# Values of the second attention for seven batches projected beside the first layer's routing, with the expert weights in other buffers and GpSimd splitting the context

## What is computed

```python
x = x + L0_attention(layernorm(x), ctx)            # 16 heads of 16
x = x + L0_experts(layernorm(x))                   # top 1 of 8 experts, 256 -> 1024 -> 256
x = x + L1_attention(layernorm(x), ctx, mask)      # 8 heads of 64, a null key and value
x = x + L1_experts(layernorm(x))                   # top 8 of 64 experts and a shared one
# inside L1_attention:
k, v = split(ctx @ Wkv, 2)                         # 361 x 512 each, per batch
q = l2norm(stable_layernorm(x) @ Wq) * q_scale
k = l2norm(k) * k_scale                            # per head; v is used as it is
```

## Time and profile before

| | |
|---|---|
| time, median of 3 runs | 731.22 us (730.6 to 733.69) |
| time of the profiled execution | 732.75 us |
| span of the profiled execution | 731.0 us |
| PE busy | 638.7 us (87%) |
| DVE busy | 391.9 us (54%) |
| ACT busy | 400.2 us (55%) |
| POOL busy | 242.0 us (33%) |
| moved by DMA | 65.11 MB, mean 89 GB/s |

### The profile page before, as it was taken

The page is one execution under the profiler, slowest core; times in us unless marked ns, Lnnn a source line. Parts: engine busy times, 40 slices in busy tenths (PEclk is TensorE's granted clock), DMA queues, the critical chain, the costliest instruction groups (busy, mean ns, idle before and its releaser), DMA issues.

```text
span 731.0 us, 15087 instructions
## 1 busy us (share of the span) xinstructions
PE 638.7 (87%) x4762; PEld 512.4 (70%) x4763; DVE 391.9 (54%) x1171; ACT 400.2 (55%) x952; POOL 242.0 (33%) x307
## 2 busy tenths in 40 slices
PE   3999889999751989998999999998696999999995
PEld 2877566666450888976878666665464999999995
DVE  5222467777643111118898745555774665566662
ACT  1454689989641333245667788686331555545442
POOL 5011455555218000001110000000044787787771
PEclk9999599999955999999999999999599999999999
DMA  6118000000086388403120010000106645555552
GB/s 146 46 31 270 7 2 2 2 2 2 1 263 214 121 282 264 149 32 85 32 53 1 8 42 1 1 2 1 32 14 170 180 141 159 155 144 148 144 143 67
DMA packets 66838, 65.11 MB, mean 89 GB/s; under 512 B 10424, under 2 KB 60373, under 8 KB 66662
## 3 DMA queue, kind: packets, MB, share of 16 engines
q1 hardware_dynamic: 62204, 58.06, 26.5%
q0 software_dynamic: 1824, 4.32, 2.3%
q10 hardware_dynamic: 2762, 2.11, 1.0%
HBM read 56.17 MB, written 8.29 MB: 88 GB/s over the span
## 4 chain that ended last, share of the span: by engine, by line
PE 69%; ACT 10%; DVE 7%; issue 5%; DMA 3%; POOL 3%; SPq 2%; DVEq 1%; POOLq 0%; ACTq 0%
ACT probs L767 4%; PE psum L1119 4%; PE psum L1106 4%; PE psum L2218 3%; PE psum L2166 3%; PE psum L2168 3%; PE psum L2167 3%; PE psum L615 3%; PE psum L629 3%; PE psum L1593 3%; PE psum L706 3%; PE psum L1615 3%; PE psum L1602 3%; DMA v_all<-in_L_ffn_W_dram 3%; PE psum L696 2%
## 5 line engine op out<-in xcount | busy, mean ns | idle before, releaser
L767 ACT ACTIVATE probs<-probs,negmax 100x361 f32<-100x361 f32 x128 | 68.9, 587 | 10.7 <-POOL probs L812 10.6
L820 DVE TENSOR_SCALAR_CACHE_REDUCE probs<-psum 100x361 f32<-100x361 f32 x128 | 60.7, 531 | 19.4 <-PE psum L696 19.4
L706 PEld LDWEIGHTS psum<-ident,probs 100*128 100x128 f32 (+1 forms) x384 | 40.4, 159 | 27.6 <-issue 20.4
L706 PE MATMUL psum<-ident,probs 100*128 100x100 f32 (+1 forms) x384 | 48.9, 266 | 11.2 <-ACT probsT L775 4.8
L1147 ACT ACTIVATE kT_all<-psum,kT_all 128x128 f32<-128x128 f32 x88 | 25.2, 369 | 51.6 <-PE psum L1106 51.6
L812 POOL TENSOR_SCALAR probs<-probs 100x722 f32<-100x722 f32 x64 | 50.5, 789 | 5.1
L2347 POOL TENSOR_TENSOR we_low<-v_all,we_high 128x512 fp32r<-128x512 f32 (+1 forms) x34 | 46.0, 1373 | 17.1 <-ACT we_high L2271 12.7
L1106 PE MATMUL psum<-kT_all,v_all 128*128 128x128 f32 x352 | 43.3, 283 | 8.5 <-DMA v_all<-in_L_ffn_W_dram 3.4
L2166 PE MATMUL psum<-xT_high,we_high 128*128 128x400 f32 x128 | 45.2, 353 | 5.5 <-DVE v_all L2411 4.1
L1106 PEld LDWEIGHTS psum<-kT_all,v_all 128*128 128x128 f32 x352 | 42.1, 198 | 11.2 <-issue 7.0
L2057 POOL TENSOR_TENSOR xT_low<-kT_all,xT_high 128x1600 fp32r<-128x1600 f32 x1 | 3.6, 3567 | 131.1 <-ACT xT_high L2034 131.1
(11 more groups left out here) (420 smaller groups left out, 1691.5 us busy)
## 6 DMA issues: line engine op xcount, KB each, us to landing
v_all<-in_L_ffn_W_dram SPq DMA_DIRECT2D x16, 1024.0 KB, 7.8
kT_all<-coefT_dram SPq DMA_DIRECT2D x18, 400.0 KB, 3.7
v_all<-in_L_ffn_Wg_dram SPq DMA_DIRECT2D x34, 128.0 KB, 2.2
v_all<-in_L_ffn_Wu_dram SPq DMA_DIRECT2D x34, 128.0 KB, 2.3
v_all<-in_L_ffn_Wd_dram SPq DMA_DIRECT2D x34, 128.0 KB, 2.3
ctx_nat<-in_ctx_dram SPq DMA_DIRECT2D x16, 192.0 KB, 2.5
xs_dram<-zeros SPq DMA_DIRECT2D x1, 2048.0 KB, 7.7
rank_rows<-rank_dram SPq DMA_DIRECT2D x18, 100.0 KB, 3.0
```

Of the source, the lines that this page charges most:

```text
L706: last = nc.tensor.transpose(pT_ps[0:rows[t], t, hh * NQ:(hh + 1) * NQ], probs[:, n % NPB, hh, t * P:t * P + rows[t]], ident[0:NQ, 0:NQ])
L767: last = nc.scalar.activation(row, row, ACT.Exp, bias=negmax[:, n % NPB, hh:hh + 1])
L820: last = nc.vector.tensor_scalar(probs[:, n % NPB, hh, 0:NKV], psum[0:NQ, n % 2 * 2 + hh, 0:NKV], -CLAMP, None, ALU.max, ALU.max, accum_ou ...
```

## The change

The value products of batches 0 to 6 move from the projections into the end of attention 0 and into the gate (`early_values`); batch 7 stays (`last_values`). They write straight to their final place in `v_all`, so the expert weights, which stood there, move to the key and query buffers (W2 in two halves). The context transposes now number sixteen instead of eight: 0 to 7 and one more before the experts (contexts 0 to 6 for values, then context 0 again for keys, then context 7 for values), and seven in the projections (contexts 1 to 7 for keys). The list `CTX1` holds this order.

Wkv is loaded at the very start and split by POOL during the first stages. In the gate POOL splits contexts 1, 2 and 3 of the list and Wq, ahead of the scatter; DVE splits 0 and 4 to 8. In the projections POOL splits all, from a full copy that ACT makes as well (`ctxT_full`), and DVE none. SP issues the biases and the weights of two experts first, then context 4, eight small transfers of the null value, and contexts 5 to 10. ACT loads the first rows (`act_first_rows`) after five batches' values and seven contexts.

```diff
 
     xnT1_ps = psum[:, 7, 0:2 * NQ].rearrange("p (c n) -> p c n", c=2)
     k1_ps = psum[:, 2:5, :]
-    v1_ps = [psum[:, k, :] for k in (6, 5, 6)]
+    CTX1 = list(range(B - 1)) + [0, B - 1] + list(range(1, B))
+    CTX_V, CTX_K = [*range(B - 1), B], [B - 1, *range(B + 1, 2 * B)]
+
+    def v1_ps(b, t):
+
+        return psum[:, t + 2 if b < B - 1 else (6, 5, 6)[t], :]
 
     def kT1_ps(b, t):
 
-        return psum[:, t % 2 + 5 if 3 * b + t < 3 * B - 4 else (3 * b + t) % 2, :]
+        return psum[:, (3 * b + t) % 2 + 5, :]
     q1_ps = psum[:, 7, :]
 
...
 
-    def sp_ctx1(sp, b, p):
-
+    def sp_ctx1(sp, n):
+
+        b, p = CTX1[n], n % 2
+        sp.wait_ge(ctxT_in_psum, CTX0 + max(n - 1, 0))
         sp_ctx(sp, b, p)
...
@@ -755,9 +770,37 @@
             b, s = m // QUADS0, m % QUADS0
             if b > 0 and s in finish:
                 finish[s](b - 1)
+            if m == M0 - 2:
+                pe.wait_ge(A0.clipped, 2 * M0)
+                transpose_ctx1(pe, 0)
         weighted(M0 - 1)
-        for s in range(3):
-            finish[s](B - 1)
+        transpose_ctx1(pe, 1)
+        finish_transpose(B - 1)
+        early_values(pe, 0, 0, 0, 3)
+        finish_transpose_back(B - 1)
+        early_values(pe, 0, 0, 3, 5)
+        early_values(pe, 0, 1, 0, 1)
...
+
+        p, cols = n % 2, slice(t * P, t * P + rows[t])
+        products = ((ctxT_high, high, 0), (ctxT_high, low, 0), (ctxT_low, high, 0), (ctxT_high, low, 1), (ctxT_low, high, 1))
+        for k in range(first, end):
+            part, w, c = products[k]
+            last = nc.tensor.matmul(ps, part[p][:, c, cols], w[:, c, :], start=(k == 0), stop=(k == 4))
+        return last
+
+    def early_values(pe, b, t, first=0, end=5):
+
+        if first == 0:
+            pe.wait_ge(ctxT_split, CTX_V[b] + 1)
+            pe.wait_ge(w1x_split, 2)
+            if b > 0:
+                pe.wait_ge(v1_stored, 3 * (b - 1) + t + 1)
+        last = times(v1_ps(b, t)[0:rows[t], :], CTX_V[b], t, wv1_high, wv1_low, first, end)
+        if end == 5:
+            last.then_inc(v1_in_psum, 1)
 
     def act_attend0(act):
...
+                split_first_ctx1(dve)
             take_tail(2 * m + 1)
             if m + 2 < M0:
...
         step(dve, nc.vector.tensor_reduce(slot_f[:, :], route_b[0:NQ], AX.X, ALU.add))
         nc.vector.tensor_copy(slot[:, :], slot_f[:, :]).then_inc(slots_ready, 1)
+        dve.wait_ge(g_exp, 1)
+        step(dve, nc.vector.tensor_reduce(top_weight[:, :], logits[:, :, :], AX.X, ALU.add))
+        step(dve, nc.vector.reciprocal(top_weight[:, :], top_weight[:, :]))
+        split_ctx1(dve, 4)
+
+    def keep_v(act, b, t):
+        act.wait_ge(v1_in_psum, 3 * b + t + 1)
+        nc.scalar.activation(v_all[0:rows[t], b, t, :], v1_ps(b, t)[0:rows[t], :], ACT.Copy).then_inc(v1_stored, 1)
 
     def act_gate(act):
+        def take_x(k):
...
+                                 xnT0_ps[k], ACT.Copy).then_inc(xnT_ready, 2)
+
+        take_ctx1(act, 1, True)
+        take_x(0)
+        take_x(1)
         act.wait_ge(ln_stats, 2 * B)
         nc.scalar.activation(std[:, B - 1:B], mv[:, B - 1:B, 1], ACT.Sqrt, bias=eps_col[0:NQ, :]).then_inc(ln_std, 1)
-        for k in range(B // 2):
-            act.wait_ge(xnT_in_psum, B + 2 * k + 2)
-            nc.scalar.activation(xnT0[:, :, 2 * k * NQ:2 * (k + 1) * NQ].rearrange("p c (b n) -> p b c n", b=2),
-                                 xnT_all_ps[k], ACT.Copy).then_inc(xnT_ready, 2)
+        keep_v(act, 0, 0)
+        take_x(2)
+        keep_v(act, 0, 1)
+        take_x(3)
+        keep_v(act, 0, 2)
+        take_ctx1(act, 2, True)
         act.wait_ge(g_centred, 1)
         nc.scalar.activation(logits[:, :, :], logits[:, :, :], ACT.Exp).then_inc(g_exp, 1)
+        for b in range(1, B - 1):
+            if b == B - 2:
+                act_first_rows(act)
+            for t in range(3):
+                keep_v(act, b, t)
+            take_ctx1(act, b + 2, b + 2 <= POOL_CTX)
...
+                for c in range(2):
+                    last = nc.tensor.transpose(xnT0_ps[k][:, b % 2, c, :], xn_all[:, b, c * P:(c + 1) * P],
+                                               ident[0:NQ, 0:NQ])
+                last.then_inc(xnT_in_psum, 1)
+
         pe.wait_ge(gate_loaded, 32)
+        xn_pair(0)
+        xn_pair(1)
+        early_values(pe, 0, 1, 1, 5)
+        xn_pair(2)
+        early_values(pe, 0, 2, 0, 2)
+        xn_pair(3)
         pe.wait_ge(A0.added, B)
-        for b in range(B):
-            pe.wait_ge(xn_ready, B + b + 1)
-            for c in range(2):
-                last = nc.tensor.transpose(xnT_all_ps[b // 2][:, b % 2, c, :], xn_all[:, b, c * P:(c + 1) * P],
-                                           ident[0:NQ, 0:NQ])
-            last.then_inc(xnT_in_psum, 1)
         for b in range(B):
             pe.wait_ge(xnT_ready, B + 2 * (b // 2) + 2)
             for c in range(2):
                 last = nc.tensor.matmul(logits_ps[:, b, :], xnT0[:, c, b * NQ:(b + 1) * NQ], wg0[:, c, :],
                                         start=(c == 0), stop=(c == 1))
             last.then_inc(gate_logits, 1)
+        early_values(pe, 0, 2, 2, 5)
+        transpose_ctx1(pe, 2)
 
         pe.wait_ge(choice_ready, 1)
         nc.tensor.matmul(ranks_ps, earlier[:, :], choice[:, :, :], start=True, stop=True)
         nc.tensor.matmul(totals_ps, ones_sq[:, :], choice[:, :, :], start=True, stop=True).then_inc(ranks_ready, 1)
+        for b in range(1, B - 1):
+            if b > 1:
+                transpose_ctx1(pe, b + 1)
+            if b == B - 2:
+                pe.wait_ge(slots_ready, 2)
+                pe.wait_ge(biases_loaded, 32)
+                nc.tensor.transpose(b1_ps, b1_rows[:, :], ident[0:E0 * HC, 0:E0 * HC]).then_inc(b1_in_psum, 1)
+            for t in range(3):
+                if b == B - 2 and t == FULL:
+                    take_rows0(pe, 0)
+                early_values(pe, b, t)
+        transpose_ctx1(pe, B)
 
     def pool_dispatch(pool):
+        split_ctx1_full(pool, 1)
+        pool.wait_ge(w1x_loaded, 16 * 7)
+        pool.wait_ge(A0.added, B)
+        pool_high(pool, wq1_high, wq1)
+        pool_low(pool, wq1, wq1_high, wq1_low, 7)
+        for n in range(2, POOL_CTX + 1):
+            split_ctx1_full(pool, n)
         pool.wait_ge(slots_ready, 2)
...
         gather(0)
         gather(1)
-        for b in range(B - 2):
+        split_ctx1_full(pool, CTX_K[1])
+        for b in range(2):
             pool.wait_ge(x2_added, b + 1)
             gather(b + 2)
+        for b in range(2, B):
+            split_ctx1_full(pool, CTX_K[b])
+            if b + 2 < B:
+                pool.wait_ge(x2_added, b + 1)
+                gather(b + 2)
 
...
@@ -1454,15 +1554,9 @@
                 query_transposes(b - 1)
             context(b + 1)
             key_transposes(b - 1, 2)
-            values(b, 0)
-            if b > 1:
-                x_transposes(b)
-                values(b, 1)
-            else:
+            if b == 1:
                 query_transposes(b - 1)
-                values(b, 1)
-                x_transposes(b)
-            values(b, 2)
+            x_transposes(b)
             queries(b)
...
@@ -1470,14 +1564,11 @@
         key_transposes(b - 1, 1)
         query_transposes(b - 1)
         key_transposes(b - 1, 2)
-        values(b, 0)
         x_transposes(b)
-        values(b, 1)
         key_transposes(b, 0)
+        queries(b)
         key_transposes(b, 1)
-        queries(b)
         key_transposes(b, 2)
-        values(b, 2)
         pe.wait_ge(null_k_stored, 1)
         pair_scores1(pe, 0)
         pe.wait_ge(kT1_stored, 3 * B)
```

More of the change, by code:

```diff
@@ L115, in build @@
     at_k, at_v = [0], [0]
-    w1_e = [carve(vals_arena, at_v, (2, H0)) for _ in range(2)]
-    w2_e = [carve(vals_arena, at_v, (HC, D)) for _ in range(2)]
     xn_all = carve(keys_arena, at_k, (B, D))[0:NQ]
@@ L155, in build @@
     two = lambda v: v[:, 0:1024].rearrange("p (c n) -> p c n", c=2)
-    wk1, wv1 = (two(vals_arena[:, 6 * SLOT_V + k * 1024:]) for k in range(2))
-    wq1 = two(vals_arena[:, 6 * SLOT_V + 2048:])
+    wk1, wv1 = (two(keys_arena[:, wkv1_at + k * 1024:]) for k in range(2))
+    wq1 = two(keys_arena[:, wq1_at:])
     wq1_high = two(nc.alloc_sbuf_tensor_at("wq1_high", [P, 1024], F32R, offset=early_at)[:, :])
@@ L487, in sp_load0 @@
             sp.dma_start(dst, src).then_inc(wo0_loaded, 16)
+        for w, at in ((wk1, 0), (wv1, 512)):
+            src = a["L1_xattn_Wkv"][:, at:at + 512]
+            sp.dma_start(w[:, 0, :], src[0:P, :]).then_inc(w1x_loaded, 16)
+            for k in range(2):
+                sp.dma_start(w[k * DREST:(k + 1) * DREST, 1, :], src[P:DC, :]).then_inc(w1x_loaded, 16)
     def sp_ctx(sp, b, p):
@@ L1081, in sp_experts, with transpose_ctx1 @@
         load(1, 1)
-        each_block(sp, block)
-    def transpose_ctx1(pe, p, loaded):
-        pe.wait_ge(ctx_loaded[p], 32 * (B // 2 + 1 - p) + 2 * loaded)
+        sp_ctx1(sp, 4)
+        for h in range(8):
```

(20 more changed lines are left out.)

225 lines of the change are left out of this document (107 added, 118 removed).

## The result

The changed kernel takes **743.6 us** (median of four runs, 739.9 to 743.8), against 731.5 for the kernel before: ratio 1.0149, 95% interval 1.011 to 1.0188 (the ratio is taken over all runs; the two medians alone give 1.0165). It is slower, and 2.6 us above the forecast of 741. The profiled execution has a span of 742.0 us, 11.0 more than before.

What follows compares the result with a forecast made beforehand. DVE was taken as nearly as late as PE, so its chain and a falling clock set the passes. 732.75 + 1.0 (gate) + 8.9 (projections) = 742.6, on the median's scale 741; range 729 to 747, the forecast's own 736 to 747.

Steps and rivals of the forecast that it cites:

- What sets a pass: Projections: a chain through DVE, not PE's work, sets the pass, so it shrinks only to 10.4 us.
- The chain: Projections: keys, ACT's squares, DVE's key reduction to x, then the query and the next keys: 10.35 us, say 10.4.
- The clock falls: Projections: PE's idle gap of about 2.5 us costs the clock in each pass, 1.4 us each; chance 0.60.
- Batch 1: Projections, pass of batch 1: the same gap, longer, costs +1.4 us.
- First batch: Projections: keys of batch 1 wait for POOL's split behind ACT's two copies, +0.5 us.
- Last pass: End of the projections: +0.95 us for the order of transposes and +1.0 for half clock.
- The 0.95 for the order: Last pass: transposes of key tile 1 behind the query, taken by ACT before squaring it, delay attention 1 by 0.95 us.
- the 1.0 for a half clock: Last pass: its query and transposes run at half clock, +1.0 us (0 to 1.7).
- The gate: Between attention 0 and experts: context 4 lands at about 219 and comes last; net +1.0 us (-4 to +4).
- POOL's hold on DVE: Gate: DVE instructions with two SBUF inputs blocked while GpSimd reads SBUF; routing chain loses up to 1.7 us.
- Block 0: First expert block: starts near 239.2 instead of 236.47, +2.7 us.
- its clock: Block 0 at 2.4 GHz needs 3.76 instead of 5.48 us, -1.7.

Runs made afterwards that it cites:

- experiment 3: The kernel before, with the values of batches 1 to 6 left out of the projections and made nowhere: 738.9 us, ratio 1.0102.
- Experiment 1: The changed kernel with 16 idle matmuls of 256 columns behind the transposes of x in passes 1 to 6: 737.4 us, ratio 1.0062 to the kernel before.
- experiment 5: The changed kernel with the transposes of key tile 1 of the last batch back ahead of the query: 737.9 us in one run.
- experiment 4: The changed kernel without POOL arithmetic from the normalising of x to the slots; DVE splits contexts 2 and 3: 740.5 us, ratio 1.0115 to the kernel before.

## Why the prediction was right, and where its terms were off

- **What sets a pass: right.** The chain was put at 10.35 to 10.4; it took 10.36 to 10.40 us wherever the clock held, in every kernel run here, the one before without its values among them (experiment 3).
- **The clock falls: right, at 1.5 a fall instead of 1.4, and in four of five passes.** "1.0 us longer, five times" = +5.0 measured +4.0: four times +1.1 and once -0.4. Experiment 1 gives 6 us back by filling the gap and nothing else. By the rule of the Trainium skill (TensorE: Matmul & The Clock Gate, HAM oscillation) the clock would hold over a gap of this size; with waits of 2.29 and 0.44 us it fell in four passes of five. The section behind it there (A second HAM failure mode: psum-queue depth-cycling) tells of a kernel in which short idling between groups of matmuls cost the clock as well; experiment 3 shows the like here, with no wait above 1.36 us.
- **Batch 1: +1.4, measured +1.4. First batch: +0.5, measured +0.4.**
- **Last pass: mechanism right, half its size.** The 0.95 for the order measured 0.94 (experiment 5); the 1.0 for a half clock was 0 in this execution.
- **The gate: the step that failed.** I wrote that context 4 comes last, that PE has done values 1 and 2 by 216 and waits, and that the scatter starts 1 us earlier. In the trace PE hardly waits for a context, and the scatter starts 4.1 us later: POOL's splits held up four DVE instructions for 6.1 us (1.45, 2.1, 1.36, 1.22), two of them ahead of PE's last transposes of x. PE waited 3.62 us there, and the logits behind it took 4.25 us instead of 2.91 (experiment 4). That makes the 4.9 us by which PE came to context 4 later than forecast, at 220.89 instead of 216. The transfer itself was put about right: 219 forecast; here it landed before 220.89, and in experiment 4, where PE waits for it, at 218. I had put POOL's hold on DVE at up to 1.7 in a sentence beside the sum, for DVE instructions with two SBUF inputs. The section that I named (the Trainium skill, SBUF — State Buffer, Who interferes with whom) also lists `copy`, `cast` and `tensor_scalar`, where their operands allow it, and excepts `tensor_reduce`; the trace agrees with each: L959, L1012 and L1029 were held, L1028 was not (0.22 us inside POOL's 1.77). I had applied half of it. Copy L1179, 6.13 us in the earlier trace rows, is of the listed kind, and I took it only as a sign of contention.
- **Block 0: +2.7 forecast, +4.0 measured, of which the gate makes +4.7; its clock: -1.7 forecast, -1.4 measured over the experts.** Net +3.3 instead of +1.0.
- **The rest: +1.8, forecast 0.** From the first transposed probabilities to the end the kernels are the same; over the twelve profiled executions of this study this part takes 311.4 to 314.0 us, without a link to the edits that I can see (before 312.2, after 313.9). What moves is the granted clock behind attention 1: 0.66 before (520 to 540) against 0.62 after (529.2 to 549.2, the same 9.2 us later as the stage), and 0.91 (560 to 580) against 0.83 (569.2 to 589.2). Why stays open.

So against the profiled spans the sum came out only 1.1 us low (+9.9 forecast, +11.0 measured; 2.6 by the medians), and that closeness is luck, because errors cancelled: the projections 2.2 under their +8.9 and the stages ahead of the gate 0.7 under, the gate and experts 2.3 over, the rest 1.8 over.

In the passes the like happens off the chain, and to the kind of instruction that I had named, one with two SBUF inputs. Row of DVE in the pass in which the clock held:

```profile
385.75 1.26 DVE L1410 SCALAR_TENSOR_TENSOR x<-probs,top_weight,x 100x256 f32<-100x256 f32 x1
```

L1410 stands behind the x that the query waits for. It took 1.26 us beside POOL's split (385.00 to 386.73) against 0.47 in the kernel before, and this pass was 10.39 all the same. The slack is used up, though: DVE's 0.23 us of waiting before the next key reduction is gone.
